# Transposed exponentials of three units in sixteen: copied out of PSUM by VectorE instead of ScalarE, with a semaphore of their own

## The reference, cut to what matters

```python
scores = jnp.einsum('bhqd,bhkd->bhqk', q, k) / scale
scores = scores + (c2p + p2c) / scale          # relative positions
probs = jax.nn.softmax(scores, axis=-1)
ctx = jnp.einsum('bhqk,bhkd->bhqd', probs, v)
out = ctx @ Wo + bo + hidden_states            # then layer norm
```

## Time and profile before

| | us |
|---|---|
| median of 3 runs | 2737.05 (2734.18 to 2737.12) |
| the profiled execution: its own time | 2735.33 |
| the profiled execution: span from first to last instruction | 2733.6 |
| busy in the span: PE, ACT, DVE, POOL | 2375.6, 2270.4, 2129.8, 577.6 |
| attention stage, from the first scores of block 0 to the end of block 15 | some 67 to 840 |

### The profile page before, as it was taken

How to read it: one execution, slowest core, us unless ns; L and a number is a source line. 1 busy time by engine, 2 the same in 40 slices (tenths; PEclk the granted TensorE clock), 3 DMA queues, 4 the chain that set the end, 5 groups by cost and what they waited for, 6 DMA issues and landing times. The chain is left out here.

```text
span 2733.6 us, 64386 instructions
## 1 busy us (share of the span) xinstructions
PE 2375.6 (87%) x18133; PEld 1298.0 (47%) x18133; DVE 2129.8 (78%) x6451; ACT 2270.4 (83%) x4511; POOL 577.6 (21%) x435
## 2 busy tenths in 40 slices
PE   3888888888883478555999999999999999999997
PEld 2666665666662256233444444444444444444443
DVE  4778888788775766954788888888888888888886
ACT  2899999989993533266999999999999999999996
POOL 3233242332420011233111111111111111111114
PEclk6999999999996589876999999999999999999999
DMA  4231222312211000000111111111111111111112
GB/s 112 53 77 44 68 58 51 75 45 67 58 43 46 1 0 0 31 0 1 47 52 57 46 46 46 46 52 57 46 46 46 46 53 56 46 46 46 46 52 87
DMA packets 195627, 129.61 MB, mean 47 GB/s; under 512 B 26667, under 2 KB 184443, under 8 KB 195579
## 3 DMA queue, kind: packets, MB, share of 16 engines
q1 hardware_dynamic: 195579, 129.02, 17.9%
HBM read 78.10 MB, written 4.73 MB: 30 GB/s over the span
## 5 line engine op out<-in xcount | busy, mean ns | idle before, releaser
L2002 DVE TENSOR_TENSOR c_Hl<-c_HF,c_Hh 128x512 f16<-128x512 f32 x1028 | 679.4, 688 | 161.5 <-ACT c_Hh L1889 145.1
L1885 ACT ACTIVATE c_HF<-c_H,c_b 128x512 f32<-128x512 f32 x1028 | 710.6, 691 | 64.2 <-PE c_H L1824 44.0
L1889 ACT ACTIVATE c_Hh<-c_H,c_b 128x512 f16<-128x512 f32 x1028 | 706.2, 687 | 0.0
L1940 POOL TENSOR_TENSOR c_EX<-c_euler,c_D 128x16 f32<-128x16 f32 x65 | 188.7, 2902 | 1194.1 <-DVE c_D L1975 1194.1
L1823 PE MATMUL c_H<-c_Cl,SH 128*128 128x512 f16 x1028 | 390.2, 380 | 0.0
L1822 PE MATMUL c_H<-c_Ch,SH 128*128 128x512 f16 x1028 | 390.2, 380 | 0.0
L1824 PE MATMUL c_H<-c_Ch,SH 128*128 128x512 f16 x1028 | 390.0, 379 | 0.0
L1833 PE MATMUL c_Y<-c_Hh,SH 128*128 128x512 f16 x1024 | 388.1, 379 | 0.1
L1835 PE MATMUL c_Y<-c_Hl,SH 128*128 128x512 f16 x1024 | 388.1, 379 | 0.0
L1834 PE MATMUL c_Y<-c_Hh,SH 128*128 128x512 f16 x1024 | 388.1, 379 | 0.0
L649 ACT ACTIVATE a_E<-a_T,a_nm 128x128 f32<-128x128 f32 x1024 | 325.3, 395 | 27.6 <-DVE a_nm L741 26.2
(11 more groups left out here) (296 smaller groups left out, 4076.2 us busy)
## 6 DMA issues: line engine op xcount, KB each, us to landing
c_CWB<-c_rows SPq DMA_DIRECT2D x260, 256.0 KB, 4.0
a_AB<-a_ST SPq DMA_DIRECT2D x256, 128.0 KB, 2.4
a_QN<-a_QH SPq DMA_DIRECT2D x128, 32.0 KB, 1.9
a_KN<-a_KH SPq DMA_DIRECT2D x128, 32.0 KB, 1.9
out<-d_O SPq DMA_DIRECT2D x16, 256.0 KB, 2.3
a_QN<-a_QL SPq DMA_DIRECT2D x64, 32.0 KB, 1.9
a_KN<-a_KL SPq DMA_DIRECT2D x64, 32.0 KB, 1.9
CUR<-in_ctx SPq DMA_DIRECT2D x1, 1848.0 KB
```

Of the source, the lines that this page charges most:

```text
L1885: act.activation(HF[:, k % 4, :], bH[k % 4][:, :], ACT.Gelu_apprx_tanh, bias=b1[:, g % EXPERTS, f:f + 1], scale=1.0 / WSCALE).then_inc(hf_ ...
L1889: act.activation(Hh[:, g % 2, f, :], bH[k % 4][:, :], ACT.Gelu_apprx_tanh, bias=b1[:, g % EXPERTS, f:f + 1], scale=1.0 / WSCALE).then_inc( ...
L2002: dve.tensor_tensor(Hl[:, g % 2, f, :], HF[:, k % 4, :], Hh[:, g % 2, f, :], ALU.subtract)\
```

## The change

The copies of units 5, 7 and 9 leave ScalarE and go to VectorE, in the same steps (8, 10 and 12), behind that step's `add_positions` and softmax work and ahead of its layer-norm step and `split_rows`. `et_ok` now counts 13 copies in a block, and the new `ed_ok` counts three. TensorE's three kinds of wait pick the semaphore by the unit, through `columns_done`.

```diff
+DVE_ET = (5, 7, 9)
+ACT_ET = tuple(w for w in range(UNITS) if w not in DVE_ET)
...
-        et_ok = Count(sem("et_ok"), UNITS, credit=2)
+        et_ok = Count(sem("et_ok"), len(ACT_ET), credit=2)
+        ed_ok = Count(sem("ed_ok"), len(DVE_ET))
...
+            def columns_done(i, w):
+                if w in DVE_ET:
+                    pe.wait_ge(ed_ok.sem, ed_ok.at(i, DVE_ET.index(w) + 1))
+                else:
+                    pe.wait_ge(et_ok.sem, et_ok.at(i, ACT_ET.index(w) + 1))
+
             def exp_transposes(i, w):
                 pe.wait_ge(e_ok.sem, e_ok.at(i, w + 1))
                 if w < 2:
                     pe.wait_ge(on_ok.sem, on_ok.at(i, 0))
                 else:
-                    pe.wait_ge(et_ok.sem, et_ok.at(i, w - 1))
+                    columns_done(i, w - 2)
...
             def out_rows(i, b, last):
                 pe.wait_ge(oc_ok.sem, oc_ok.at(i, b + 1))
                 if b >= 2:
-                    pe.wait_ge(et_ok.sem, et_ok.at(i, UNITS - 3 + b))
+                    columns_done(i, UNITS - 4 + b)
...
             def weighted_values(i, w):
                 b, g = w // UPB, w % UPB
-                pe.wait_ge(et_ok.sem, et_ok.at(i, w + 1))
+                columns_done(i, w)
...
             # ScalarE's body
                 for u in range(UNITS + TAIL):
-                    if 0 <= u - 3 < UNITS:
+                    if u - 3 in ACT_ET:
                         exp_columns(i, u - 3)
...
             # VectorE
+            def exp_columns(i, w):
+                dve.wait_ge(et_ps.sem, et_ps.at(i, w + 1))
+                dve.wait_ge(pv.sem, pv.at(i, w - 2))
+                dve.tensor_copy(ET[:, w % 3, :, :], bE[w % 2][:, :].rearrange("p (h s) -> p h s", h=HG))\
+                    .then_inc(ed_ok.sem, 1)
...
                     for b in range(NB):
                         if u == OUT_NORM[b]:
                             softmax_outputs(i, b)
+                    if u - 3 in DVE_ET:
+                        exp_columns(i, u - 3)
                     if u in (2, 3) and not last:
                         low_half(i, 1, u - 2)
```

## The result

Time after: **2741.80 us** median of 20 runs (2737.67 to 2745.21), against 2737.16 in the 20 runs of the kernel before that go with them. The ratio is 1.0017, with a 95% interval of 1.0010 to 1.0023: slower by some 4.6 us. Two of the 20 runs before took 2943 and 6817 us and are left out of the ratio. The forecast was 2744.5, and "slower" for a difference above 0.2%, or 5.5 us: the direction was right, the size too large, and by the prediction's own 5.5 us the result falls to "same", to which it had given 0.36.

The account below looks back on a forecast made before the run. A ring between TensorE and ScalarE bounds the attention stage, TensorE pacing value-projection steps. 14 x 0.57 + 0.25 - 0.7 = +7.5 us gives 2742.8; the median, 1.7 higher, is 2744.5, with an 8-in-10 range of 2735 to 2750.

Parts of the forecast that it names:

- Unit 7: Steady block, step 8: TensorE's transposes of unit 7 start 0.51 us later, behind VectorE's copy of unit 5.
- Units 8 and 9: Steady block: TensorE's transposes of unit 8 start 0.17 us later, those of unit 9 0.30 later behind unit 7's copy.
- Unit 11: Steady block, step 12: TensorE's transposes of unit 11 start 0.57 us later, behind VectorE's copy of unit 9.
- rival 3: Faster: TensorE's wait before unit 8's transposes goes, 0.34 us a block, everything behind follows; total 2731 us, chance 0.13.
- Unit 15 and the block: End of a steady block: unit 13's copy, 0.57 us later, holds back unit 15's transposes; the block grows by 0.57.
- the chain from scores 14: Block end: unit 14's scores, then additions of 14 and 15, exponentials of 15 and unit 13's copy, all 0.57 us late.
- the cushion: Block end: unit 13's copy ends 0.09 us ahead of need of unit 15's transposes, counted with a start of 0.14.
- Block 15: Last block, no bucket tiles or value projections: TensorE waits for ScalarE, whose freed time helps, half of 1.44 us: -0.7.
- Block 0: First block, no layer norm of a previous block: only the DMA path counts, +0.25 us.
- The DMA path: Split of tile 7, eight DMAs, chunk 0: 0.25 us late in a steady block, covered by the 0.57.
- Rival 1: Only the DMA path moves the block's end: 0.25 us a block, +3.1 in all, total 2740 us, chance 0.20.
- Rival 2: VectorE's contiguous copy takes 0.40 us, not 0.68; a block does not change, total 2736 us, chance 0.08.

Follow-up runs that it names:

- split semaphore alone: Changed kernel with all 16 copies back on ScalarE, the second semaphore `ed_ok` kept; measured 2737.02 us, ratio 1.0005 to the kernel before.
- four copies: Changed kernel with VectorE copying units 5, 6, 8 and 10, each one step earlier (step w+2); measured 2732.00 us, ratio 0.9975.
- the load: Kernel before, plus a VectorE instruction of about the copy's length at the three copy places, which nobody waits for; measured 2738.35 us, ratio 1.0004.

## Why the prediction was right or wrong

**The mechanism held.** Except at unit 9, the prediction's order of events is in the trace: VectorE's copy behind the additions, the long wait before unit 7 (1.16, forecast 1.2), the later bucket products, ScalarE's waits before the high rows in steps 9, 10 and 12, the split without its wait in steps 8 and 12, the later additions of units 14 and 15. In step 10 the split still waits, 0.19. Of the three waits named for TensorE, those of 0.2 before units 9 and 11 do not show as idle time. One step earlier the same copies gain, with equal load and equal semaphores, so it is the moment of the copy that costs.

**Unit 7: +0.51 forecast, +0.44 measured.** The 0.07 is TensorE's start behind the copy, for which I had carried over 0.14 from the earlier trace rows; it is 0.05 in the changed kernel (copy 430.78 + 0.69, transposes 431.52), and the copy ends 0.02 later than forecast. The split semaphore alone gives the same 0.05.

**Units 8 and 9: +0.17 and +0.30 forecast, +0.12 and +0.13 measured.** Unit 8 inherits the error of unit 7. For unit 9 the prediction had "end 433.71, transposes of unit 9 at 433.85", +0.30, with the copy of unit 7 as the cause. The copy comes 0.09 sooner in the block than I had it (22.95 against 23.04 us after the first scores), and the start 0.09 sooner behind it (434.95 + 0.69 = 435.64, start 435.69). That is also where TensorE's own work puts it: from T8 to T9 it is 2.36 here, 2.38 with the split semaphore alone and 2.37 with the copies ahead of the additions, where no copy is late. So the +0.13 is the shift of unit 8 handed on, and the late copy of unit 7 adds nothing that can be seen.

**Unit 11: +0.57 forecast, +0.43 measured.** Of the 0.14, 0.09 is once more the start behind the copy, the rest the start of the copy (27.89 against 27.95). What the sum did not show is how little of this comes from the first two copies. With unit 9 alone T11 is at 28.61, with all three at 28.63, with units 5 and 7 at 28.40. The last copy sets T11 by itself, because VectorE's step 12 hangs on ScalarE's step 11, and TensorE has no idle time left behind unit 8, so a shift there goes on to the units behind it; of the 0.44 at unit 7 only 0.12 is left at unit 8, where the room of 0.34 that rival 3 works out (the wait of 0.18 and what stands in it) takes the rest.

**Unit 15 and the block: +0.57 forecast, +0.33 measured.** The additions and exponentials of unit 15 are about 0.5 late, as the chain from scores 14 says, but T15 only 0.33. The term that failed is the cushion. I had found 0.09 between the copy of unit 13 and what T15 needs, and then not taken it off: by the prediction's own numbers a steady block was 0.57 - 0.09 = 0.48 longer. The cushion was also counted with the start of 0.14; with 0.05 it is 0.18 (446.78 - 0.05 - 446.55). 0.51 less 0.18 is 0.33. So of the 0.24 too much, 0.09 is this slip, 0.09 the start behind the copy, and 0.06 the smaller shift. This is the main sizing error, 14 x 0.24 = 3.4 us.

**Block 15: -0.7 forecast, about +0.5 measured** (blocks 14 and 15 together +0.89, less 0.33 for block 14). The sign was wrong. I reasoned that ScalarE is the pacemaker there and that its freed time must help. The timeline of TensorE in block 15 of the changed kernel, transposes of units 7, 9 and 11:

```profile
819.70 0.63 PE L494 MATMUL a_E<-a_ident,a_E 128*128 128x128 f32 x4 [0.23 <-DVE a_ET L759]
...
823.41 0.63 PE L494 MATMUL a_E<-a_ident,a_E 128*128 128x128 f32 x4 [0.44 <-DVE a_ET L759]
...
827.13 0.63 PE L494 MATMUL a_E<-a_ident,a_E 128*128 128x128 f32 x4 [0.45 <-DVE a_ET L759]
```

It waits for VectorE's copy at all three. Against the block 15 of before, counted from its first scores, the transposes of unit 7 are not late (15.39, before 15.44), those of unit 9 are (19.11, before 18.73), those of unit 11 (22.82, before 22.51) and of unit 15 (30.30, before 29.81). The copy is late in its step there too; I had applied the rule of the steady block to every block but this one. The kernels with early copies show what I had in mind: T15 of block 15 is at 29.28 with units 5, 7 and 9 one step earlier and at 29.09 with the copies ahead of the additions, 0.53 and 0.72 sooner than before. So the -0.7 was about right for ScalarE's freed time alone; what it lacked was the lateness. That is 1.2 us of the sum, in the other direction from the main error.

**Block 0: +0.25 forecast, -0.14 measured.** Here the two executions differ before the change can act. The granted TensorE clock is half of full speed until 72.9 in the execution of before and until 72.1 in that of after, and the first transposes of block 0, ahead of any moved copy, already stand 0.31 sooner from the first scores. From there the block lost about 0.17. Block 1 took +0.65: chunk 0 is held by the softmax outputs, and these come 0.27 later than in a steady block. The errors of block 15 (1.2 too little) and of the steady blocks (3.4 too much) took off part of each other; that part of the nearness to 2744.5 is luck.

**The DMA path.** The split of tile 7 was forecast 0.25 late and covered. It is only 0.08 late (28.56 us after the first scores, 28.48 before), and covered: chunk 0 waits 0.25 for the softmax outputs and not for the DMA. Rival 1's 2740 is nearer to the result than the forecast's 2744.5, yet its mechanism is out: the block is set by T15, which is late by more than chunk 0 (0.33 against 0.19). Rival 2 is out by the copy's 0.685, rival 3 by T8, which comes later and not earlier. What rival 3 described, an earlier T8 and all behind it, is real, and is what the kernel with units 6, 8 and 10 one step earlier gains; it forecast 0.34 a block for it, and 0.58 came.

**What stays open.** No run moved the copies in the loop but not in block 15. The cause of the 2 us by which the untouched rest of the program differs between executions is open too.

## What to carry to other kernels

When work moves to an engine with idle time, its length is the smaller question; the larger one is at what point of the step it now ends, and who waits for it. Here three copies lose 0.33 us a block; the same three gain 0.16 one step earlier, and three others 0.58. Look for the last wait before the stretch in which the pacemaker (here TensorE) has none: lateness ahead of it is partly soaked up, lateness behind it goes through nearly in full, and the copy that ends that wait is the one to bring forward.

## What the runs showed of the hardware

**The start behind a semaphore is not one number.** TensorE's transposes start 0.14 us after the copy that releases them in the kernel before and 0.05 in the loop of the changed one, for VectorE's copies and for ScalarE's. The kernel with the split semaphore alone does it too. But with unit 9 alone on VectorE its transposes again start 0.14 behind (439.73 + 0.69 = 440.42, start 440.56), and so they do in block 15 of the changed kernel (818.87 + 0.69 = 819.56, start 819.70). The 0.05 goes with transposes of 0.65 to 0.66 us, the 0.14 with 0.63.

The full trace shows what goes with it. The program has two semaphore waits ahead of these transposes. Where the start is 0.14, TensorE's queue holds a semaphore instruction of its own just ahead of the transposes; where it is 0.05, there is none. Over all kernels, of 1104 such starts (those that waited over 0.1 us for a copy), 811 have no such instruction, and all start 0.05 to 0.06 behind; 293 have one, and 292 of them start 0.14 to 0.15 behind. It holds within one kernel too: with unit 9 alone the instruction stands ahead of units 11 and 15 and not ahead of 2 to 8, and only the former start 0.14 behind. The kernel before has 1041 of these instructions on TensorE in all, the changed one 845, 196 fewer, as many as 14 for each of the 14 blocks of the loop; its register instructions grow from 2984 to 3208. Why the split semaphore removes them was not tried.

**Single long blocks.** Several kernels have a block that is 1.4 to 3.3 us too long, mostly block 0 or 1: 51.5 (block 0, unit 6 one step earlier; its block 1 49.85), 50.91 (block 1, ahead of the additions), 50.67 and 50.49 (block 1, both triples one step earlier), 50.2 (block 1, split semaphore alone), 49.87 and 50.43 (blocks 0 and 1, four copies), and now and then one inside the loop (50.10 with the split semaphore, 50.15 and 50.16 under the load). The kernel before and the changed one show none. In each of these eleven blocks the granted clock of TensorE falls to half for one stretch of 3.4 us. The only other such stretch in blocks 0 to 14, once block 0 has come to the full clock, is at the end of block 0 with units 5 and 7, a block of 49.55. Stretches of the split-semaphore kernel, columns as in the first line; the first is the same place one block before the second:

```profile
core 0: us, PE busy (x) PEld busy (x) DVE busy (x) ACT busy (x) POOL busy (x), PEclk, DMA share, GB/s
591.75:595.15 3.40, 2.09 (x54) 1.37 (x53) 2.13 (x11) 2.71 (x8) 3.40 (x2) 1.00 0.37 82
640.40:643.80 3.40, 2.04 (x51) 1.33 (x53) 2.09 (x11) 2.67 (x8) 3.40 (x2) 0.99 0.37 84
643.80:647.20 3.40, 3.40 (x54) 2.16 (x54) 1.41 (x3) 2.94 (x7) 3.40 (x3) 0.50 0.00 0
```

The same two matmuls of an output product, one block apart, at the full and at the half clock:

```profile
595.36 0.49 PE L529 MATMUL a_M<-a_Wo,a_OT 128*128 128x128 f32 x2
...
644.26 0.80 PE L529 MATMUL a_M<-a_Wo,a_OT 128*128 128x128 f32 x2
```

Laid over an undisturbed block of the loop, this block is level until 643.8, falls behind step by step up to 1.44 us at 647.2, and stays there: the stretch is the whole of its excess. What makes the clock fall is not shown. TensorE was busy for 2.04 of the 3.4 us ahead of the fall, and for 2.09 in the same place one block before, where the clock did not fall. In blocks 0 and 1 a longer wait of chunk 0 comes on top, for instance in block 0 with unit 6 one step earlier, where a steady block has 0.58:

```profile
106.15 0.43 PE L466 MATMUL a_G<-a_AB,a_window 64*128 64x64 f16 x16 [3.29 <-DMA a_AB<-a_ST]
```

Why the DMA comes late there is open. The blocks explain the profiled executions; how often such a stretch falls into the other runs was not recorded. The unit 6 kernel should be 14 x 0.47 = 6.6 us faster by its steady blocks and is 4.8 by the medians.
